# First operand's rows loaded by three transfers of 24 rows in place of one with a leading broadcast

## What is computed

```
q, k, v = proj(LN(x), Wq, bq), proj(LN(x), Wk, bk), proj(LN(x), Wv, bv)   # 4 x 16 heads x 512 x 8
q, k    = rope(q), rope(k)
scores  = q @ k^T / sqrt(8), masked to the causal triangle
out     = softmax(scores) @ v @ Wo.T + bo
x       = x + out
```

## Time and profile before

| | us |
|---|---|
| median of 3 runs | 688.79 (686.36 to 688.85) |
| profiled execution, its own time | 690.77 |
| its span in the trace | 689.0 |
| PE busy | 516.5 (75%) |
| DVE busy | 377.3 (55%) |
| ACT busy | 253.2 (37%) |
| POOL busy | 318.0 (46%) |

### The profile page before, as it was taken

One profiled execution on the slowest core, in us unless ns is written; L12 is line 12 of the kernel. 1 busy time (PEld: TensorE's weight loads), 2 busy tenths in 40 slices (PEclk: granted clock), 3 DMA queues, 4 the chain that ended last, 5 costly groups with the idle time before them and its releaser, 6 DMA issues. The chain is left out here.

```text
span 689.0 us, 12192 instructions
## 1 busy us (share of the span) xinstructions
PE 516.5 (75%) x3527; PEld 355.4 (52%) x3528; DVE 377.3 (55%) x1247; ACT 253.2 (37%) x519; POOL 318.0 (46%) x373
## 2 busy tenths in 40 slices
PE   3994699999999867577992089899679610699970
PEld 1442344554655336576992044545447510699970
DVE  3864546888887744452442548741745771244433
ACT  1312345767766733232446133101023110344432
POOL 1454035965254762364543485145321476155553
PEclk9997757999999989898997589999879855699995
DMA  6154103214322114233435000000000013122216
GB/s 176 47 183 147 49 1 84 76 48 128 109 68 64 55 42 120 59 105 103 110 110 142 1 0 0 1 0 1 0 1 0 21 54 81 44 71 71 70 50 183
DMA packets 45992, 46.11 MB, mean 67 GB/s; under 512 B 8133, under 2 KB 39424, under 8 KB 45792
## 3 DMA queue, kind: packets, MB, share of 16 engines
q1 hardware_dynamic: 37440, 31.48, 16.7%
q0 software_dynamic: 4544, 9.35, 4.1%
q10 hardware_dynamic: 3952, 4.59, 2.0%
HBM read 31.68 MB, written 15.12 MB: 68 GB/s over the span
## 5 line engine op out<-in xcount | busy, mean ns | idle before, releaser
L1282 ACT ACTIVATE store<-ps 128x512 f32<-128x512 f32 x160 | 91.5, 595 | 55.4 <-PE ps L850 55.1
L1070 DVE TENSOR_REDUCE at_mx<-ps 128x1 f32<-128x512 f32 (+1 forms) x128 | 74.1, 617 | 29.8 <-PE ps L837 29.5
L835 PE MATMUL ps<-at_hats 72*128 72x512 bf16 (+3 forms) x256 | 75.2, 331 | 11.8 <-DVE at_mx L1070 10.1
L1367 POOL TENSOR_SCALAR_AFFINE_SELECT store<-store 128x512 f32<-128x512 f32 x64 | 39.0, 635 | 72.5 <-ACT store L1282 72.4
L850 PE MATMUL ps<-at_hats 74*128 74x512 bf16 (+3 forms) x256 | 66.9, 328 | 6.5 <-DMA at_hats<-at_mT 6.5
L461 POOL DMA_INDIRECT expert_rows<-r_rows,r_sloti x64 | 62.2, 972 | 19.1 <-issue 18.1
L597 POOL DMA_INDIRECT expert_results<-at_vall x39 | 37.5, 961 | 54.6 <-DVE at_vall L539 32.7
L597 POOL DMA_INDIRECT expert_results<-moe_y,moe_targeti x39 | 37.4, 958 | 49.0 <-DVE moe_y L539 46.0
L837 PE MATMUL ps<-c_mask_q_bf,c_ident_bf 128*128 128x128 bf16 x256 | 54.1, 236 | 0.0
L867 PE MATMUL ps<-store,at_vext 128*32 128x128 f32 (+3 forms) x512 | 51.7, 482 | 0.5 <-ACT at_oT_more L1250 0.5
L571 PE MATMUL ps<-at_vall,at_hats 128*128 128x128 f32 x312 | 44.7, 290 | 7.1 <-issue 4.1
(11 more groups left out here) (313 smaller groups left out, 1048.6 us busy)
## 6 DMA issues: line engine op xcount, KB each, us to landing
at_hats<-parts SPq DMA_DIRECT2D x32, 288.0 KB
moe_w<-moe_w_dram SPq DMA_DIRECT2D x8, 512.0 KB, 6.0
store<-ssm_tables_dram SPq DMA_DIRECT2D x35, 86.0 KB
at_vall<-expert_rows SPq DMA_DIRECT2D x39, 64.5 KB
moe_xg<-expert_rows SPq DMA_DIRECT2D x39, 64.5 KB
at_hats<-expert_results SPq DMA_DIRECT2D x8, 256.0 KB, 5.1
moe_ytok<-expert_results SPq DMA_DIRECT2D x8, 256.0 KB, 4.9
parts<-store ACTq DMA_DIRECT2D x12, 128.0 KB
```

The lines of the kernel that those rows point to most:

```text
L835: pe.matmul(bankA(n)[:, col:col + (t + 1) * P], hatq[0:MROW, slot, h, t * P:(t + 1) * P], hatk[0:MROW, slot, h, 0:(t + 1) * P], start=True ...
L1070: m = dve.tensor_reduce(mx[:, u % 2, t, h:h + 1], bankA(n)[:, 0:(t + 1) * P], AX.X, ALU.max)
L1282: act.activation(pt[:, u % 2, j // 2, S * (j % 2):S * (j % 2 + 1)], bankB(n), ACT.Exp).then_inc(s_e, 1)
L1367: pool.affine_select(out=own, in_=own, compare_op=ALU.is_ge, fill=0.0, base=0, pattern=[[0, HG], [1, P]], channel_multiplier=-1).then_inc( ...
```

## The change

Line 1411's one transfer into 72 partitions becomes three transfers into 24 partitions each, all from the same 24 rows of `parts` and with no broadcast axis. They land in the same bytes. The load of `hatk` stays. A unit now adds 64 to `s_hat[slot]` where it added 32, and PE's wait follows.

```diff
@@ a_chunk
                 if k == 0:
-                    pe.wait_ge(s_hat[slot], 32 * (u // SLOTS + 1))
+                    pe.wait_ge(s_hat[slot], 64 * (u // SLOTS + 1))
@@ load_hats
-                sp.dma_start(hatq[0:MROW, slot, :, :], bc(q, 3, 0)).then_inc(s_hat[slot], 16)
+                for r in range(3):
+                    sp.dma_start(hatq[3 * DH * r:3 * DH * (r + 1), slot, :, :], q).then_inc(s_hat[slot], 16)
                 sp.dma_start(hatk[0:MROW, slot, :, :], bc(k, 3, 1)).then_inc(s_hat[slot], 16)
```

## The result

The changed kernel takes 0.967 of the time of the kernel before (95% interval 0.959 to 0.976): a median of 666.65 us against 687.58. One of its four executions took 825.29 us: it counts in this median but not in the ratio, and the other three have a median of 665.39 us. Run again beside the experiments it takes 0.971 (0.966 to 0.975), 666.57 us. The forecast was 658.3 us, in a range of 653 to 674: the sign and the range held, but the gain was put at 30.5 us and is about 21. The profiled execution took 667.91 us, its span is 666.2 us against 689.0, so 22.8 us less.

What follows compares the result with a forecast made beforehand. The prediction took the narrow q load on three DMA engines, delaying stores and max_row(0), to bound the kernel through two stalls and a lowered clock. Gains 8.9 + 3.0 + 5.7 + 10.7 + 2.2 = 30.5 us gave 658.3 us, range 653 to 674.

Steps and rivals of the forecast that it cites:

- its own case: Whole kernel: the forecast without the rivals, 658.3 us, range 654 to 664, chance 0.80.
- signs of being right: DMA plateau of 0.19 gone, ACT's wait under 1 us, chunk (0,3) at 51.6, first b_chunk 62.5 to 63, full clock.
- signs of being wrong: A 0.19 plateau that stays, a clock of 0.5 in the loop, or max_row(3)'s shift not found at the span's end.
- Who holds the DMA engines: Loads before the loop: line 1411 is spread over three engines at 26 GB/s each, thirteen idle; new transfers use twelve.
- Issues on SP's queue: SP's loads: two more issues per unit at 0.75 us each, 3.1 us per unit, costing nothing while covered.
- First stall: PE before chunk (0,3), behind ACT's wait for stores of `parts`: start at 51.6 instead of 60.46, 8.9 us gained.
- Clock before the loop: Chunks (0,3) to (1,0): at full clock 4.2 us instead of 7.2, 3.0 us gained.
- Second stall: PE's wait for max_row(0) before the first b_chunk: goes whole, 5.7 us gained, with 0.5 to 2.4 us to spare.
- Clock in the loop: Loop's first units at full clock: 10.7 us gained from max_row(1) to max_row(3), 2.2 us at the start.
- Everything behind the loop's third unit shifts whole: After the loop's third unit: the lead stays to the end, with some 3 us either way for the clock's falls.
- The clock falls at the loop's start all the same: Rival at the loop's start: first units again take 14 us, only 14.6 or 17.6 us won, 671 to 674; chance 0.13.
- The split changes nothing: Rival for the q loads: the three pieces use the same engines as the one did, time stays 688.8 us; chance 0.04.

Runs made afterwards that it cites:

- e1_columns: Kernel before, its q load cut by columns into three transfers, each still into 72 partitions with the leading broadcast of three: 1.001, 691.51 us.
- e6_rows_12_12: Changed kernel with each copy of q's rows loaded by two transfers of 12 rows, six q transfers per unit: 0.987, 676.56 us.
- e7_rows_17_7: Changed kernel with each copy of q's rows loaded by two transfers, of 17 and 7 rows, six per unit: 1.084, 742.47 us.
- e4_order_wide: Changed kernel, SP's loads of units 2 and 3 behind the stores of batch 1, max_row(0) ahead of unit 4's load: 0.959, 663.99 us.
- e2_clock_held: Kernel before with 9 more dummy matmuls in each of PE's two stalls, loads untouched: 0.988, 683.06 us.
- e3_order_narrow: Kernel before, q load unaltered, SP's loads of units 2 and 3 behind batch 1's stores, max_row(0) ahead of unit 4's load: 0.978, 676.81 us.

## Why the prediction was right, and where its size was off

**The range was met, in part by its width.** For its own case, without the rivals, the prediction gave 654 to 664 us; 666.65 lies outside. It lies in 653 to 674 because that range was stretched to take in a rival, the clock falling at the loop's start, that didn't happen. Of its own signs of being right, the vanished plateau and the full clock from 50 to 120 us came true; ACT's wait (5.0 us, not under 1), chunk (0,3) (53.67, not 51.6) and the first b_chunk (66.57, not 62.5 to 63) did not. One of its signs of being wrong did: a part of the shift at `max_row(3)` is gone at the end of the span. The mechanism was right; what follows is where the sum was off.

**Who holds the DMA engines: right.** The plateau of 0.19 to 0.20 was line 1411. Cutting without widening keeps it (e1_columns), the row count at the front alone makes a load fast or very slow (e6_rows_12_12, e7_rows_17_7), and with 24 rows it is gone.

**Issues on SP's queue: too dear, and then nearly too cheap.** An issue of 24 rows takes 0.37 us (1.14 us for three), half of the 0.75 taken; a unit takes 2.2 us and not 3.1 as long as the engines keep up (unit 6, behind a backlog, took 4.7: from 55.10 to 59.84). "Covered" was right, but e6_rows_12_12 shows how little cover there was.

**First stall: 8.9 us forecast, 6.8 measured** (60.46 to 53.67). Of the 2.1 us missing, 0.8 is a later preparation in this execution (the dummy block at 47.82 instead of 47.01), and 1.3 is the wait that PE still has. The failed term is the landing of the stores of batch 1, put at 46 us and measured at 50.80. The prediction took the twelve engines to be loaded to 60% by SP: 1.9 us of moving, at 26 GB/s per engine, in 3.1 us of issuing. Both were off. A unit is issued in 2.2 us, and at the 21 GB/s per busy engine of the windows above its 590,000 bytes take an estimated 2.3 us on twelve engines. (The prediction's own have 246 GB/s at a share of 0.79: more than twelve engines' worth of work, at 19 GB/s each, and not ten at 26.) So the loads came as fast as the engines could carry them, and the stores had to share: from 38 to 50 us the DMA share is 0.7 to 0.9. e4_order_wide, with two units less beside them, has the stores landed 5.1 us sooner after their issue and starts the loop some 2 us sooner.

**Clock before the loop: 3.0 forecast, 2.7 measured** (7.2 to 58.19 - 53.67 = 4.5).

**Second stall: 5.7 forecast, 4.1 measured.** From chunk (1,0) to the first b_chunk it took 80.13 - 67.69 = 12.4 us and now takes 66.57 - 58.19 = 8.4. Of the 1.6 us missing, 1.2 are PE waiting for DVE's negated maxima (60.55): DVE's step of line 1078 took 1.10 us where it had taken 0.17. It now coincides with POOL's additions to x of line 1345, which before had ended by then. First the kernel before, then the changed one:

```profile
62.02 4.92 POOL L1345 TENSOR_TENSOR x<-x,at_w_bo 128x512 f32<-128x512 f32 x4
...
68.40 0.17 DVE L1078 TENSOR_SCALAR at_mh<-at_mx 128x16 bf16<-128x16 f32 x1
```

```profile
55.23 4.93 POOL L1345 TENSOR_TENSOR x<-x,at_w_bo 128x512 f32<-128x512 f32 x4
...
59.09 1.10 DVE L1078 TENSOR_SCALAR at_mh<-at_mx 128x16 bf16<-128x16 f32 x1
```

DVE's step ends 0.03 us behind POOL's last addition (60.19 and 60.16). The same holds in all nine traces in which the two meet, where the step takes 0.82 to 1.11 us; in the three in which POOL had ended (before, e1_columns, e7_rows_17_7) it takes 0.17. So in these traces the step ends only once POOL has; what holds it is not shown. The prediction moved DVE's work forward without asking what it would then run beside; no run changed this alone. The other 0.5 is the wait for `max_row(0)`: it reached PE 5.0 us after its issue (61.58 to 66.57), where the prediction allowed 2.0 to 3.9. It had taken the engines to be nearly free by then, but the DMA share from 56 to 64 us is still 0.76 to 0.93, with the loads of units 4 to 6 and the stores of batch 3. The forecast's margin of 0.5 to 2.4 us at this place was used up.

**The two as separate terms: a wrong picture with a right sum.** The prediction adds 8.9 and 5.7 as two gains. e1_columns shows that they are one: as the first shrank, the second grew by as much. The sum came out because the change removes the backlog behind both; for a change that helps only one of them the same working would have promised time that isn't there.

**Clock in the loop: 12.9 forecast, 13.0 measured** in the changed kernel (154.3 to 141.3), and 12.9 with the clock alone held up (e2_clock_held). This was the largest term and the one most in doubt. Of its two parts the start, from the first b_chunk to `max_row(1)`, gave 1.6 us (6.95 to 71.88 - 66.57 = 5.31; 71.88 is the second of the three issues in the row of 61.58) where 2.2 were forecast, and the next two units 11.4 (28.06 to 88.58 - 71.88 = 16.70) where 10.7 were.

**"Everything behind the loop's third unit shifts whole": this failed.** From `max_row(3)` to the end of the span 3.8 us of the lead of 26.6 are lost, 3.4 of them in the spectral transposes, where the clock falls a second time. The prediction allowed 3 us either way and put the middle at zero. Three traces of kernels with a shorter attention have 27.5 to 27.6 us there (changed, changed again, e2_clock_held), the others without dummies there 24.2 to 26.2, and two executions of one kernel 24.2 and 26.2. The stretch's length follows the clock in all of them, as the table's last column shows. Whether the new timing makes the second fall likelier, or three traces agree by chance, stays open.

Of the 30.5 us, then, 26.6 were there at `max_row(3)`, 22.8 at the end of the span; the medians differ by 20.9.

**The rivals.** "The clock falls at the loop's start all the same" didn't happen here, but it happened in e3_order_narrow and e6_rows_12_12, from stalls of 3.9 and 4.0 us at just that place, at 677 us in both. "The split changes nothing" fell. The Trainium skill's advice against splitting by partitions ("DMA: Bandwidth & Descriptors", section "Rules for kernel authors") holds where the pieces get the engines that the whole had, and e6_rows_12_12 is such a case: 24 rows cut into 12 and 12 gained nothing and cost 10 us. It doesn't where the cut raises the leading count, as in the change itself. The rule on the number of engines in the Trainium skill, "DMA: Bandwidth & Descriptors", section "Why a DMA increments its semaphore by 16 and not by 1", agrees with the plateau at 0.19 to 0.20 and, by their times, with e6_rows_12_12 and e7_rows_17_7.

## What to carry to other kernels

When DMA engines look idle while someone waits for a DMA, compare the share with small sixteenths: the plateau at 3/16 was one transfer on three engines, and what was small and urgent on those engines stood behind it. And once the loads are spread, ask again whether the engines keep up with the issues: here they did so barely, at 21 GB/s each under load and not the 26 that three of them had shown alone. Price the backlog and not the waits: list everyone who waits on it, for removing one wait moves the time to the next, and end the list only with the last bytes, the other queue's stores among them. A stall of 4 us on PE cost more than twice itself here (10 us in e6_rows_12_12), because the clock stayed down in the units that followed.

## What was not expected of the hardware

The issue of 24 rows without a broadcast takes 0.37 us, that of 72 rows with one 0.70: three issues moved the same bytes for 1.14 us of SP's queue. And with q loads in runs of 1.3 to 1.4 KB instead of 4 KB, on the same three engines, the other queue's stores, in pieces of 1 KB, landed 6 us sooner (51.3 instead of 57.6 us, e1_columns), while the loads themselves ended no sooner. Whether that is the size of the pieces or SP's slower issuing, which put the later loads out only after the stores (unit 3's from 47.77 us on), this run doesn't tell apart.
